# Sets of K of 4, 8, 8, 8 and 4 heads, six early pairs of x, and a new order into the output tiles

## What is computed

```python
# x: (128, 32, 512); H = 32 heads, N = 64 modes, L = 512
dt = exp(log_dt)                                   # (32,)
A = -exp(log_A_real) + 1j * A_imag                 # (32, 64)
Ct = (C[..., 0] + 1j * C[..., 1]) * (exp(A * dt[:, None]) - 1) / A
K = 2 * einsum('hn,hnl->hl', Ct, exp((A * dt[:, None])[:, :, None] * arange(512))).real
y = irfft(rfft(x, 1024) * rfft(K, 1024))[..., :512] + x * D[:, None]    # causal convolution
x = x + y * (arange(512)[None, :] < length[:, None])[:, None, :]
h = einsum('bsd,brd->bsr', x, lora_A[ids])         # rank 16, one of 32 adapters for each b
x = x + einsum('bsd,od->bso', x, W) + bias + einsum('bsr,bor->bso', h, lora_B[ids])
```

## Time and profile before

| | us |
|---|---|
| median of 3 runs (lowest, highest) | 216.61 (216.46, 216.75) |
| the profiled execution | 218.4 |
| its span, first to last instruction | 216.4 |
| TensorE busy | 193.1 (89%) |
| DVE busy | 169.8 (78%) |
| ACT busy | 116.1 (54%) |
| POOL busy | 89.9 (42%) |
| DMA, mean over the span | 260 GB/s |

### The profile page before, as it was taken

One profiled execution on the slowest core, in us unless ns is written; L12 is line 12 of the kernel. 1 busy time (PEld: TensorE's weight loads), 2 busy tenths in 40 slices (PEclk: granted clock), 3 DMA queues, 4 the chain that ended last, 5 costly groups with the idle time before them and its releaser, 6 DMA issues.

```text
span 216.4 us, 4328 instructions
## 1 busy us (share of the span) xinstructions
PE 193.1 (89%) x1046; PEld 167.0 (77%) x1046; DVE 169.8 (78%) x364; ACT 116.1 (54%) x330; POOL 89.9 (42%) x144
## 2 busy tenths in 40 slices
PE   0057999997999999499999999999999999999992
PEld 0045899996999999488888888888888888888881
DVE  3897888679699876479888887878787888878652
ACT  2747362552555234457756566666667575656520
...
GB/s 142 289 291 157 391 405 407 409 408 410 408 411 407 374 262 323 407 179 178 277 201 218 205 224 200 227 201 214 217 194 228 207 208 211 223 195 185 101 106 133
DMA packets 21520, 56.46 MB, mean 261 GB/s; under 512 B 3394, under 2 KB 3842, under 8 KB 21250
## 3 DMA queue, kind: packets, MB, share of 16 engines
...
q0 software_dynamic: 2560, 8.39, 13.8%
...
HBM read 45.64 MB, written 10.65 MB: 260 GB/s over the span
## 4 chain that ended last, share of the span: by engine, by line
PE 73%; DMA 7%; DVE 7%; POOL 5%; issue 3%; ACT 2%; SPq 1%; DVEq 0%; ACTq 0%; POOLq 0%
PE y_ps L934 21%; PE k_ps L934 21%; PE z_ps L895 17%; PE z_ps L920 7%; DMA w_sb<-w_t 3%; DMA strip<-k_pad 2%; PE y_ps L943 2%; PE y_ps L944 2%; PE k_ps L943 2%; PE k_ps L944 2%; POOL w_lo L381 2%; DVE z_all L725 1%; DVE xp L719 1%; DVE work L684 1%; DMA tab<-table 1%
## 5 line engine op out<-in xcount | busy, mean ns | idle before, releaser
L895 PE MATMUL z_ps<-xp,strip 128*128 128x512 f32 (+3 forms) x384 | 64.9, 331 | 0.3 <-DMA strip<-k_pad 0.3
L895 PEld LDWEIGHTS z_ps<-xp,strip 128*128 128x128 f32 x384 | 60.6, 200 | 4.5 <-DMA strip<-k_pad 0.4
L406 POOL DMA_INDIRECT b_hl<-b_tab,b_idx x32 | 39.2, 1225 | 10.2 <-issue 9.8
L934 PE MATMUL y_ps<-w_hi,xp 128*128 128x512 f32 x128 | 43.2, 399 | 0.0
L934 PE MATMUL k_ps<-w_hi,xp 128*128 128x512 f32 x128 | 42.6, 393 | 0.0
L401 POOL CAST ag<-a_hl 128x128 fp32r x64 | 23.1, 363 | 41.4 <-PE z_ps L920 30.2
L521 ACT ACTIVATE ag<-a_hl 128x64 fp32r x128 | 25.8, 250 | 22.1 <-issue 22.1
L439 ACT ACTIVATE xp<-z_all 128x512 fp32r<-128x512 f32 x32 | 20.0, 629 | 26.8 <-PE z_ps L895 25.0
L719 DVE TENSOR_TENSOR xp<-z_all,xp 128x512 fp32r<-128x512 f32 x32 | 25.8, 807 | 4.8 <-ACT xp L439 4.5
L934 PEld LDWEIGHTS y_ps<-w_hi,xp 128*128 128x128 f32 x128 | 24.6, 192 | 4.9
L725 DVE TENSOR_TENSOR z_all<-z_ps,mask 128x512 f32<-128x512 f32 (+2 forms) x33 | 22.2, 672 | 7.5 <-PE z_ps L895 7.2
...
## 6 DMA issues: line engine op xcount, KB each, us to landing
strip<-k_pad SPq DMA_DIRECT2D x31, 512.0 KB, 8.4
z_all<-x_conv SPq DMA_DIRECT2D x16, 512.0 KB, 9.4
x_t<-x_tile SPq DMA_DIRECT2D x32, 256.0 KB, 2.7
out<-a_raw SPq DMA_DIRECT2D x32, 256.0 KB
a_raw<-a_t SPq DMA_DIRECT2D x2, 512.0 KB, 9.6
x_t<-b_rows SPq DMA_DIRECT2D x2, 512.0 KB, 10.6
w_sb<-w_t SPq DMA_DIRECT2D x2, 512.0 KB, 7.1
b_tab<-b_hl SPq DMA_DIRECT2D x1, 1024.0 KB, 10.6
```

Of the source, the lines that this page charges most:

```text
L406: g.indirect_dma_start(out=b_hl[:, t % BS, :].bitcast(F32), out_offset=None, in_=b_tab, in_offset=bass.IndirectOffsetOnAxis(ap=b_idx[:, t: ...
L895: last = nc.tensor.matmul(z_ps[:, h % ZS, m * P:L], strip[:, h % SS, m * P:(m + 1) * P, t], xp[:, h % XS, 0:LC - m, e, :], start=(n == 0), ...
L934: last = nc.tensor.matmul(y_bank(s), xp[:, s % XS, c, e, :], w[:, c, :], start=(n == 0), stop=False)
```

## The change

The sets of K are 4, 8, 8, 8 and 4 heads. Six pairs of x are loaded ahead of the strips, not seven, and nearly all that SP issues among the strips stands at other heads. ACT makes the exponentials of heads 12 to 31 by one instruction for each head, four at each of heads 5 to 9; before, DVE made the exponents of 24 heads at once and ACT one exponential of them. `log_dt` comes by a transfer of its own on ACT's queue; lengths come spread over rows; the row constants are a column of the table. POOL makes three coefficients in two steps, not four in four, and DVE combines them in four instructions for two. The halves of W are loaded at heads 28 and 30, and the first x tile at head 30. The first tile has its own order on TensorE, ACT gathers two tiles ahead of W's split, POOL adds ones to the last two parts of W ahead of the lo part of the second, and the wait for the bias is moved to its first use.

The diff, cut to its core:

```diff
-GROUPS = ((0, 8), (8, 16), (16, 24), (24, 32))
+GROUPS = ((0, 4), (4, 12), (12, 20), (20, 28), (28, 32))
-PRE = 7
-X_AT = {5: 7, 7: 8, 10: 9, 13: 10, 15: 11, 17: 12, 19: 13, 21: 14, 23: 15}
-IDS_AT = 6
-A_AT, B_AT = {9: 0, 12: 1}, {16: 0, 18: 1}
-SPLIT_A = {14: 0, 15: 1, 18: 2, 19: 3}
+PRE = 6
+X_AT = {5: 6, 7: 7, 9: 8, 10: 9, 12: 10, 14: 11, 16: 12, 18: 13, 20: 14, 22: 15}
+IDS_AT = 4
+A_AT, B_AT, W_AT = {8: 0, 11: 1}, {13: 0, 15: 1}, {28: 0, 30: 1}
+XT_AT = 30
+SPLIT_A = {17: 0, 18: 1, 19: 2, 20: 3}
 SPLIT_B = {21: 0, 22: 1, 23: 2, 24: 3}
-K_AFTER = {2: 7, 3: 14}
-WARM_0, WARM_1 = 12, 2
-STEPS_AT = {2: (4, 5, 6, 7, 8, 9), 3: (11, 12, 13, 14, 15, 16)}
+K_AFTER = {2: 5, 3: 11, 4: 15}
+WARM_0, WARM_1 = 13, 3
+STEPS_AT = {2: (3, 3, 4, 5, 6, 7), 3: (8, 9, 10, 11, 12, 13), 4: (14, 14, 15, 15, 16, 16)}
+MAG_FIRST = 5
+MAGS_AT = {5: (12, 16), 6: (16, 20), 7: (20, 24), 8: (24, 28), 9: (28, 32)}
...
-            link(g.tensor_tensor(mm[:, 0, 0, :], sm[:, 4, :], sm[:, 6, :], ALU.subtract))
-            link(g.tensor_tensor(mm[:, 0, 1, :], sm[:, 5, :], sm[:, 7, :], ALU.add))
-            link(g.tensor_tensor(mm[:, 1, 1, :], sm[:, 6, :], sm[:, 4, :], ALU.subtract))
-            link(g.tensor_tensor(mm[:, 1, 0, :], sm[:, 5, :], sm[:, 7, :], ALU.add))
+            link(g.tensor_tensor(mm[:, 0:3:2, :], both_ends(sm[:, 4, :]), both_ends(sm[:, 6, :]), ALU.subtract))
+            link(g.tensor_tensor(mm[:, 1, :], sm[:, 5, :], sm[:, 7, :], ALU.add))
...
+            act.dma_start(log_dt[:, :], log_steps).then_inc(dt_in, 16)
...
-            split_x(1)
-            group_store(0)
-            group_sines(1)
-            magnitudes(GROUPS[1][0], NH, 1)
+            magnitudes_of(GROUPS[1][0], MAG_FIRST)
+            group_store(0)
+            magnitudes(MAG_FIRST, GROUPS[1][1], 1)
+            group_sines(1)
+            split_x(1)
             split_x(2)
             group_store(1)
...
+                if h in MAGS_AT:
+                    magnitudes_of(*MAGS_AT[h])
...
             gather(0, 0)
+            gather(1, 1)
             split_w(0)
             split_w(1)
...
-            gather(1, 1)
+            x1_hi(1, 1, True)
             h_down(0, 0)
-            x1_hi(1, 1, True)
...
-            for c in range(LC):
-                pool.wait_ge(w_in[c // 2], 16)
-                d = w_sb[:, c, c * P:(c + 1) * P]
-                g.tensor_tensor(d, d, eye[:, :], ALU.add).then_inc(w_eye, 1)
-                if c % 2:
-                    split_w(c - 1)
-                    split_w(c)
+            add_ones(0)
+            add_ones(1)
+            split_w(0)
+            add_ones(2)
+            add_ones(3)
+            split_w(1)
+            split_w(2)
+            split_w(3)
...
+            turns()
             k_low(0)
+            phases()
+            whole()
             fraction()
-            exponents_of(GROUPS[1][0], NH)
             remainder(0)
-            remainder(1)
             multiply()
             scale()
+            remainder(1)
             k_low(1)
...
-            dve.wait_ge(bias_in, 16)
             dve.wait_ge(z_masked, NH + 1)
             x1_of(1, 1, 0)
+            x1_remainder(1, 1)
             h_masked(0, 0)
-            x1_remainder(1, 1)
...
+            def first_tile():
+
+                pe.wait_ge(xhi_early, 1)
+                pe.wait_ge(xhi_done, 1)
+                for c in range(LC):
+                    pe.wait_ge(w_hi_done, c + 1)
+                    nc.tensor.matmul(y_bank(0), xp[:, 0, c, 0, :], w_hi[:, c, :], start=(c == 0), stop=False)
...
-            pe.wait_ge(xlo_early, 1)
-            tile_h(0, 0, True)
-            tile_base(0, 0, True)
+            first_tile()
```

97 lines of the change are left out of this document (61 added, 36 removed).

## The result

The changed kernel takes **218.07 us** (median of 16 runs, 216.86 to 220.52), the kernel before 216.67 (16 runs beside them). The ratio is 1.0053, 95% interval 1.0029 to 1.0077: half a per cent slower, where 213.7 us and "faster" was forecast. The profiled execution took 216.86 us with a span of 215.1, and is the fastest of its 16.

The account below looks back on a forecast made before the run. TensorE and the transfer queue just behind it were taken to bound the convolution. Setup -1.5, convolution +1.3 and transition -2.7 took the span from 216.4 to 213.5 us; with 2.0 outside it and 1.8 off for the median, 213.7 (range 211.0 to 215.9).

Parts of the forecast that it names:

- Part 1, the setup: Up to the first heads: shorter coefficients and a four-head first set start heads at 19.65, not 21.12; 1.5 us gained.
- Part 2, strip 4: At head 4: strip 4 waits for the second store, landing at 24.4; strip lands at 28.6, TensorE waits 0.8 us.
- (a): At strip 4: the second store is served at once in 1.7 us, strip 2.9 us earlier; 210.8 us in all; chance 0.12.
- (b): At strip 4: the second store takes 6.5 us as before, strip at 30.6, +2.0; 215.7 us in all; chance 0.12.
- Part 3, the convolution: Heads 4 to 31: transfers set the pace to head 17 at 59.6; end at 89.0, where it was 89.17.
- 1.9 us of low clock: Convolution: low clock behind the 1.5 us gap at 51.94, ahead of the fourth set, was to go with that gap.
- Part 4, the transition: From convolution to tiles: earlier loads and new orders start tile 2 at 97.65, not 100.57; transition term -2.7 us.
- rival (c): Ahead of the first tile: the clock falls in the 0.9 us gap at 89.0; 214.6 us in all; chance 0.09.
- Rival (e): At strip 12: ACT's late second set delays its store and starves the queue; slower, 217.3 us or above; chance 0.08.

Follow-up runs that it names:

- coefs_tiles: tiles_only plus the shorter coefficients and the step sizes on their own transfer, sets of K as before: 216.65 us, 0.9973 of the kernel before.
- less_x: The changed kernel without the loads of x pairs 7, 9, 11, 13 and 15: 221.35 us, 1.0175 of the kernel before.
- tiles_only: The kernel before with only the edits of the transition to the tiles: 215.34 us, 0.9922 of the kernel before.
- ones_a_behind: tiles_only with the edits of both ones_first and a_behind: 214.21 us, 0.9894 of the kernel before.
- a_behind: tiles_only with ACT's and POOL's splits of A moved behind the factors of the fourth set: 214.27 us, 0.9872 of the kernel before.
- ones_first: tiles_only with POOL's ones of W's second half ahead of its first lo part: 214.32 us, 0.9885 of the kernel before.
- gather_late: The changed kernel with ACT's gather of the second tile back behind the last piece of x: 217.50 us, 1.0035 of the kernel before.

## Why the prediction was wrong, step by step

**Part 1, the setup: right in its times, in one term by luck.** The second set's factors came at 18.12 (forecast 18.1), heads at 19.62 (19.65), the first store was served in 1.5 us (1.7). DVE first uses `ct` at 11.15 (forecast 11.1; 11.65 before). But I put that down to POOL's two steps fewer, 0.65 us, and POOL's `ez` (L363 before) came only 0.22 sooner, at 9.32. In coefs_tiles, with the same short coefficients and sets of eight, `ct` is used at 11.74. What brought it forward is likely DVE's half-wide steps ahead of it (the one at L704 took 0.43 us; 0.69 in coefs_tiles); no run tried them alone.

**Part 2, strip 4: right.** The second store went out at 19.82 and took 4.4 us:

```profile
k_pad<-k_sb ACTq DMA_DIRECT2D x1, 32.0 KB, 4.4
...
strip<-k_pad SPq DMA_DIRECT2D x1, 512.0 KB, 6.4
```

It landed at 24.3 (forecast 24.4), head 4 began at 28.63 (28.6). The Trainium skill's round-robin rule ("DMA: Bandwidth & Descriptors", section "Queues, rings and completion order") would, as I read it, have had the small store pass the strips; the 4.4 us speak against it, as the 5.5 and 6.5 of the earlier trace rows did. Rivals (a) and (b) did not come.

**Part 3, the convolution: the mechanism right, two terms wrong.** Transfers do set the pace from head 10 on, for instance 2.54 and 2.68 us a head for two transfers of 1.28. But I let the queue run at full rate from strip 4's landing on. The restart costs more: strip 5, the second row above, issued at 25.11, landed at 31.5, 2.9 us behind strip 4 where 1.6 was counted for it and the ids. Between the two strips stand the ids:

```profile
ids<-ids_all SPq DMA_DIRECT2D x1, 80.0 KB, 5.6
```

Issued at 24.64, they landed at 30.24, 1.7 us behind strip 4 where 0.3 was counted, and from there the transfers follow at 1.28 us again. It isn't the ids' own landing that costs: in less_x they landed 0.3 us behind strip 4, and strip 5 still 3.4 behind it. What would happen with the ids elsewhere was not tried. Head 17 came at 61.09, not 59.6; the 15 heads behind it took 29.6 us, not 29.4; and the convolution ended at 90.68, not 89.0: **+1.7 us**.

The second term is the comparison. I wrote that 1.9 us of low clock go with the gap, and took them as a gain in the span; then I took another 1.8 us off, as the distance of that profiled execution to the median. These are the same microseconds: the profiled execution lay above the median because it paid for the low clock twice, in the convolution and ahead of the tiles, where the middle group of executions (0.986 to 0.995) paid at most once, and my sum had taken both stretches away. **1.8 us were counted twice.** The comparison with an undisturbed convolution (87.35, as tiles_only shows) would have shown the convolution's end 1.7 us later by my own numbers, not 0.2 earlier, and all of the setup's gain and the gap's gone with it.

**Part 4, the transition: right in kind, too large.** From the convolution's end to tile 2 I had 97.65 - 89.0 = 8.65 us; it took 100.43 - 90.68 = 9.75, **+1.1 us**, all of it ahead of the first tile, where 0.9 us was counted and 2.15 passed. Behind that TensorE stopped once more, for 0.15 us, so POOL did not release tile 2, as I had it. ACT and POOL there:

```profile
84.41 0.40 ACT L540 ACTIVATE ag<-a_hl 128x64 fp32r x2 [0.85 <-issue]
85.67 0.41 ACT L540 ACTIVATE ag<-a_hl 128x64 fp32r x2 [0.85 <-issue]
...
88.45 1.14 ACT L532 ACTIVATE w_hi<-w_sb 128x512 fp32r<-128x512 f32 x2
...
91.30 1.15 ACT L532 ACTIVATE w_hi<-w_sb 128x512 fp32r<-128x512 f32 x2 [1.22 <-POOL w_sb L421]
92.36 0.21 ACT L584 ACTIVATE xp<-x_t 128x32 fp32r<-128x32 f32 x1
```

```profile
89.15 1.29 POOL L385 TENSOR_TENSOR w_lo<-w_sb,w_hi 128x512 fp32r<-128x512 f32 x1 [7.43 <-ACT w_hi L532]
90.40 1.27 POOL L421 TENSOR_TENSOR w_sb<-w_sb,eye 128x128 f32<-128x128 f32 x2
```

A pair of copies of a gather takes 1.26 us from start to start here, with 405 to 427 GB/s of transfers, where it took 0.76 among the tiles of the kernel before (96.92 to 97.68), so W's first hi parts start at 88.45, not near 85. And I left out the order of POOL: the ones for the third and fourth part stand behind the first lo part, ACT waits 1.22 us for them ahead of its second pair of hi parts, and the last piece of x stands behind that on ACT. By this reading 1.2 us of the 2.15 us gap are theirs; the runs bear out less, since with the ones ahead the gap was 1.51 us for 1.83 (ones_a_behind, a_behind) and in ones_first no shorter. tiles_only shows the transition's true worth, 0.85 us at full clock, for the 2.7 of my sum. The clock did not fall in this record's gap, so rival (c) did not come there.

**The tiles** were taken as unchanged; they gave back 1.2 us.

**The whole** adds up: 213.7, and 1.8 counted twice, 1.7 in the convolution, 1.1 in the transition, less 1.2 in the tiles, is 217.1, 0.2 above the profiled execution's 216.86 (its time outside the span was 1.8, not 2.0). The other 1.2 us to the median are not in this record, since it is the fastest of 16: the others have the same code and longer spans. Their cause stays open. The clock is part of it: 8 of the 16 are below 0.995, with a median span of 216.7 us for 216.0, and in gather_late, whose code is the same up to there, the clock fell behind a wait of 1.71 us for strip 4 (0.69 from 28 to 32 us). A later restart may be another: strip 5 landed up to 0.9 us later in the other records with the same order. No record of a slower execution of the change itself shows either.

Rival (e), slower through SyncE's stand at strip 12, was not what made the change slower: strip 12 was issued at 41.93, inside the 42.6 that I gave it. But the margin was right to worry about: three small edits of the order fell over it.
